# Square roots on ScalarE, two more merges on GpSimd and a new order, in a fused long-convolution and FFN kernel

## What is computed

```
q = layernorm(x)                                  # over the last axis, eps 1e-5
kv[b,i,j,h,l] = k[b,h,i,l] * k[b,h,j,l]           # k is the context; it is v too
y = causal convolution of kv along l with ssm_kernel[h]   (irfft(rfft(kv) * rfft(kernel)))
out = einsum('bijhl,bhil->bjhl', y + kv * D[h], q)
x = x + out
g = silu(W_gate layernorm(x));  u = W_up layernorm(x)     # W = (integer - 128) * scale
x = x + W_down (g * u)
```

## Time and profile before

| what | us |
|---|---|
| median of 3 runs | 76.36 |
| lowest and highest | 76.27, 76.8 |
| span of the profiled execution, first to last instruction | 74.54 (page: 74.5) |
| total of the profiled execution itself | not shown |

### The profile page before, as it was taken

The page is one execution under the profiler, slowest core; times in us unless marked ns, Lnnn a source line. Parts: engine busy times, 40 slices in busy tenths (PEclk is TensorE's granted clock), DMA queues, the critical chain, the costliest instruction groups (busy, mean ns, idle before and its releaser), DMA issues.

```text
span 74.5 us, 1494 instructions
## 1 busy us (share of the span) xinstructions
PE 69.8 (94%) x470; PEld 57.7 (77%) x470; DVE 61.7 (83%) x187; ACT 45.5 (61%) x115; POOL 58.8 (79%) x76
## 2 busy tenths in 40 slices
PE   5999989999999989999999999999999999999920
PEld 4666557988878848889798889797999989899810
DVE  0078899999988999999999899999968884586760
ACT  1503436464867879967746894657768796776400
POOL 6033587997999999899999999479998999339230
PEclk9999999999999999999999999999999999999998
DMA  0898999999997000000000000000002006000404
GB/s 8 235 254 230 372 315 364 324 382 392 361 356 224 29 0 0 0 0 4 9 0 0 0 0 4 0 0 0 0 13 70 0 0 210 1 9 0 140 1 141
DMA packets 7128, 8.29 MB, mean 111 GB/s; under 512 B 816, under 2 KB 6224, under 8 KB 7120
## 3 DMA queue, kind: packets, MB, share of 16 engines
q1 hardware_dynamic: 6768, 7.88, 33.0%
q10 hardware_dynamic: 352, 0.31, 1.2%
HBM read 7.12 MB, written 1.07 MB: 110 GB/s over the span
## 4 chain that ended last, share of the span: by engine, by line
PE 68%; POOL 16%; DVE 9%; issue 2%; ACT 1%; POOLq 0%; DVEq 0%
PE conv L1018 26%; PE down L1037 13%; POOL products L387 10%; PE conv L985 6%; PE turn L1058 5%; PE conv L994 5%; PE conv L996 5%; POOL rstd_q L371 4%; PE turn L965 3%; DVE terms L731 3%; PE turn L947 2%; PE turn L1037 2%; POOL terms L279 2%; DVE terms L734 1%; DVE terms L738 1%
## 5 line engine op out<-in xcount | busy, mean ns | idle before, releaser
L1018 PE MATMUL conv<-f_parts,wgu 128*128 128x256 f16 x176 | 22.1, 273 | 0.0
L387 POOL TENSOR_TENSOR products<-k_skip 128x512 f32<-128x512 f32 (+1 forms) x16 | 18.2, 1147 | 1.2 <-DMA k_skip<-ctx_skip 1.2
L1018 PEld LDWEIGHTS conv<-f_parts,wgu 128*128 128x128 f16 x176 | 16.6, 98 | 2.7 <-DVE hidden L746 0.2
L257 POOL TENSOR_TENSOR h_lo<-hidden,h_hi 128x256 fp32r<-128x256 f32 x18 | 13.1, 745 | 2.6 <-ACT h_hi L527 2.5
L746 DVE SCALAR_TENSOR_TENSOR hidden<-conv,su_sb,gate_act 128x256 f32<-128x256 f32 (+1 forms) x24 | 11.5, 482 | 3.0 <-ACT gate_act L522 2.8
L522 ACT ACTIVATE gate_act<-conv,sg_sb 128x256 f32<-128x256 f32 (+1 forms) x24 | 11.2, 467 | 4.2 <-PE conv L1018 3.9
L985 PE MATMUL conv<-products,toeplitz 128*128 128x288 f32 x32 | 11.3, 437 | 0.1
L731 DVE TENSOR_TENSOR terms<-conv,q_ext 128x512 f32<-128x512 f32 x16 | 10.9, 682 | 0.5 <-ACT q_ext L504 0.3
L994 PE MATMUL conv<-products,toeplitz 128*128 128x288 f32 x32 | 10.6, 413 | 0.3 <-DVE toeplitz L664 0.3
L996 PE MATMUL conv<-products,toeplitz 128*128 128x288 f32 x32 | 10.4, 406 | 0.0
L527 ACT ACTIVATE h_hi<-hidden 128x256 fp32r<-128x256 f32 x20 | 8.3, 413 | 3.4 <-DVE hidden L746 3.1
(11 more groups left out here) (64 smaller groups left out, 121.6 us busy)
## 6 DMA issues: line engine op xcount, KB each, us to landing
k_skip<-ctx_skip SPq DMA_DIRECT2D x3, 384.0 KB, 5.9
toeplitz<-taps_pad SPq DMA_DIRECT2D x2, 512.0 KB, 8.6
out<-x_sb SPq DMA_DIRECT2D x7, 128.0 KB, 1.7
toeplitz<-matrices SPq DMA_DIRECT2D x3, 256.0 KB, 5.4
wg_int<-wg_t SPq DMA_DIRECT2D x1, 704.0 KB, 7.6
wu_int<-wu_t SPq DMA_DIRECT2D x1, 704.0 KB, 8.8
wd_int<-wd_t SPq DMA_DIRECT2D x1, 640.0 KB, 10.0
x_sb<-x SPq DMA_DIRECT2D x1, 512.0 KB, 5.1
```

The source lines that it names most:

```text
L257: eng.tensor_tensor(low_of(i, t), hidden[up_lanes(t), i % 2, t, :], high_of(i, t), ALU.subtract).then_inc(done, 1)
L387: nc.gpsimd.tensor_tensor(view(products[:, n:n + 1], first * MADE + GROUP, [[MADE, halves], [GROUP, 4], [1, GROUP]]), view(k, 0, [[EXT * B ...
L1018: done = nc.tensor.matmul(bank_of(i, t)[:, n, :], wgu[:, c, column:column + P], f_parts[:, i % 2, part, c, :], start=(c == 0 and part == 0 ...
```

## The change

- The eight roots of q are taken by ScalarE's square root with eps as its bias, in four instructions (tiles 0, 1, 2 and 3, 4 to 7: `SQRT_Q`), followed by VectorE's reciprocal and one shift for each of these groups. The same holds for FFN tiles 0 and 1 (`SQRT_F`), with a shift of their own for each; GpSimd keeps the roots of FFN tiles 2 to 7. `variance_of_q` goes, and so does `variance_of_f` for tiles 0 and 1.
- ScalarE loads the square root's table at the start and Silu's between `squares(12)` and `squares(13)`, ahead of `gate(0, 0)`.
- Tile 1's front and back slots are merged on GpSimd, between `pairs(6)` and `pairs(7)`, so that its sum has 8 transposes instead of 16.
- The lists of all engines but SyncE's are in another order; `fill` has 17 matmuls instead of 18. Waits for loads stand inside the helpers now.
- GpSimd fills one more constant, eps.

The diff, cut; after what is shown the orders go on differing in the same way to the end of each list:

```diff
@@ -42,11 +42,14 @@
 HIGH_ON_DVE = []
 LOW_ON_DVE = [(LAST, 1), (LAST, 4)]
 
-UNMERGED = 2
-TWICE_MERGED = 3
-BACK_ON_POOL = [5, 6, 7]
+FRONT = {1: "pool", 2: "pool", 3: "pool", 4: "pool", 5: "pool", 6: "pool", 7: "pool"}
+BACKS = {1: "pool", 2: "dve", 3: "dve", 4: "dve", 5: "pool", 6: "pool", 7: "pool"}
+BOTH = {3: "dve", 4: "dve", 5: "dve", 6: "dve", 7: "dve"}
 
 EARLY_TURNS = 6
+
+SQRT_Q = [(0, 1), (1, 2), (2, 4), (4, TILES)]
+SQRT_F = [(0, 1), (1, 2)]
 
 
 
...
-TERM_SLOTS = [0, P, 2 * P, 3 * P, BACK, BACK + P + SPARE, BACK + 2 * (P + SPARE), CROSS]
-ONCE_SLOTS = [0, 2 * P, BACK, BACK + 2 * (P + SPARE)]
-TWICE_SLOTS = [0, BACK]
+FRONT_SLOTS = [0, P, 2 * P, 3 * P]
+BACK_SLOTS = [BACK, BACK + P + SPARE, BACK + 2 * (P + SPARE), CROSS]
+
+
+def slots_of(t):
+    if t in BOTH:
+        return [0, BACK]
+    front = FRONT_SLOTS[::2] if t in FRONT else FRONT_SLOTS
+    back = BACK_SLOTS[::2] if t in BACKS else BACK_SLOTS
+    return front + [BACK, BACK + 2 * (P + SPARE)] if t in BACKS else front + back
...
             pool.wait_ge(half_ready, 1)
-            root_q(0)
-            pool.wait_ge(k_loaded[2], 16)
             pairs(2, 0, 1)
             pairs(2, 1, 2)
-            root_q(1)
             pairs(3, 0, 1)
             pairs(3, 1, 2)
-            root_q(2)
-            pool.wait_ge(k_loaded[3], 16)
             pairs(4, 0, 2)
             pairs(5, 0, 2)
             pairs(6, 0, 2)
-            root_q(3)
+            merge_front(nc.gpsimd, 1)
+            merge_back(nc.gpsimd, 1)
             pairs(7, 0, 2)
-            root_f(0)
-            pool.wait_ge(k_loaded[4], 16)
             pairs(8, 0, 2)
+            pairs(9, 0, 2)
             merge_front(nc.gpsimd, 2)
-            root_q(4)
-            pairs(9, 0, 2)
-            root_f(1)
             pairs(10, 0, 2)
-            root_q(5)
             pairs(11, 0, 2)
-            pool.wait_ge(k_loaded[5], 16)
+            merge_front(nc.gpsimd, 3)
             pairs(12, 0, 2)
-            root_q(6)
-            merge_front(nc.gpsimd, 3)
-            root_q(7)
             merge_front(nc.gpsimd, 4)
-            low(0, 0)
             root_f(2)
             pairs(13, 0, 2)
+            low(0, 0)
+            pairs(14, 0, 2)
             root_f(3)
             low(0, 1)
+            merge_front(nc.gpsimd, 5)
+            merge_back(nc.gpsimd, 5)
+            pairs(15, 0, 2)
             low(0, 2)
-            pairs(14, 0, 2)
-            merge_front(nc.gpsimd, 5)
-            pairs(15, 0, 2)
...
+            def sqrt_q(n):
+                first, last = SQRT_Q[n]
+                act.wait_ge(q_moments, last)
+                nc.scalar.activation(std_q[:, first:last], moments_q[:, first:last, 1], ACT.Sqrt,
+                                     bias=eps[:, :]).then_inc(q_std, 1)
+
+            def sqrt_f(n):
+                first, last = SQRT_F[n]
+                act.wait_ge(f_moments, last)
+                nc.scalar.activation(std_f[:, first:last], moments_f[:, first:last, 1], ACT.Sqrt,
+                                     bias=eps[:, :]).then_inc(f_std, 1)
...
-            nc.scalar.preload_act_table(ACT.Silu)
+            nc.scalar.preload_act_table(ACT.Sqrt)
             act.wait_ge(taps_ready, 1)
             act.dma_start(taps_pad, taps_sb[:, :]).then_inc(taps_stored, 16)
+            act.wait_ge(eps_ready, 1)
+            sqrt_q(0)
             norm_q(0)
             evict_q(0)
-            act.wait_ge(k_loaded[2], 16)
+            sqrt_q(1)
             squares(2)
+            norm_q(1)
             squares(3)
-            norm_q(1)
+            squares(4)
+            evict_q(1)
+            squares(5)
             wrap(0)
-            evict_q(1)
-            act.wait_ge(k_loaded[3], 16)
-            squares(4)
+            sqrt_q(2)
             norm_q(2)
-            squares(5)
             squares(6)
             wrap(1)
+            squares(7)
+            squares(8)
+            norm_q(3)
             evict_q(2)
-            squares(7)
-            act.wait_ge(k_loaded[4], 16)
-            squares(8)
+            sqrt_q(3)
+            sqrt_f(0)
             convert_gate()
-            norm_q(3)
-            wrap(2)
-            squares(9)
             evict_q(3)
             norm_f(0)
+            squares(9)
             norm_q(4)
+            wrap(2)
+            high_f(0)
+            squares(10)
+            sqrt_f(1)
+            norm_q(5)
+            evict_q(4)
             convert_up()
-            squares(10)
-            high_f(0)
-            evict_q(4)
             norm_f(1)
+            wrap(3)
+            evict_q(5)
             squares(11)
-            wrap(3)
             high_f(1)
-            norm_q(5)
+            squares(12)
+            load_silu()
+            squares(13)
+            gate(0, 0)
+            squares(14)
+            wrap(4)
+            hidden_high(0, 0)
+            gate(0, 1)
+            norm_q(6)
             convert_down()
-            evict_q(5)
-            act.wait_ge(scales_loaded, 3 * 16)
-            gate(0, 0)
-            wrap(4)
-            gate(0, 1)
-            hidden_high(0, 0)
-            norm_q(6)
+            gate(0, 2)
...
+            def rstd_of_q(n):
+                first, last = SQRT_Q[n]
+                dve.wait_ge(q_std, n + 1)
+                dve.reciprocal(rstd_q[:, first:last], std_q[:, first:last]).then_inc(q_rstd, 1)
+
+            def shift_of_q(n):
+                first, last = SQRT_Q[n]
+                dve.wait_ge(q_rstd, n + 1)
+                dve.scalar_tensor_tensor(out=shift_q[:, first:last], in0=moments_q[:, first:last, 0], scalar=-1.0,
+                                         in1=rstd_q[:, first:last], op0=ALU.mult,
+                                         op1=ALU.mult).then_inc(q_shift, last - first)
...
+            def rstd_of_f(n):
+                first, last = SQRT_F[n]
+                dve.wait_ge(f_std, n + 1)
+                dve.reciprocal(rstd_f[:, first:last], std_f[:, first:last]).then_inc(f_rstd, last - first)
+
             def shift_of_f(t):
-                wait(dve, f_rstd, t + 1)
+                if t < len(SQRT_F):
+                    dve.wait_ge(f_rstd, t + 1)
+                else:
+                    wait(dve, pool_f_rstd, t + 1 - len(SQRT_F))
...
-            dve.wait_ge(x_loaded[0], 16)
+            all_products(0, 0, 1)
             stats_of_q(0)
-            dve.wait_ge(k_loaded[0], 16)
-            all_products(0, 0, 1)
             moments_of_q(0)
             all_products(0, 1, 2)
-            dve.wait_ge(anti_ready, 1)
-            dve.wait_ge(direct_loaded[0], 16)
             direct(0)
-            variance_of_q(0)
+            rstd_of_q(0)
             shift_of_q(0)
-            dve.wait_ge(k_loaded[1], 16)
             all_products(1, 0, 1)
+            direct(1)
             all_products(1, 1, 2)
-            dve.wait_ge(direct_loaded[1], 16)
-            direct(1)
-            dve.wait_ge(x_loaded[1], 16)
             stats_of_q(1)
             moments_of_q(1)
             multiply_terms(0)
-            variance_of_q(1)
-            dve.wait_ge(direct_loaded[2], 16)
+            rstd_of_q(1)
+            shift_of_q(1)
             direct(2)
+            multiply_terms(1)
+            stats_of_q(2)
+            stats_of_q(3)
             direct(3)
-            dve.wait_ge(x_loaded[2], 16)
-            stats_of_q(2)
-            shift_of_q(1)
             moments_of_q(2)
-            multiply_terms(1)
-            variance_of_q(2)
-            stats_of_q(3)
-            dve.wait_ge(direct_loaded[3], 16)
+            moments_of_q(3)
             direct(4)
+            multiply_terms(2)
+            rstd_of_q(2)
             direct(5)
             shift_of_q(2)
-            moments_of_q(3)
-            multiply_terms(2)
-            variance_of_q(3)
             multiply_terms(3)
+            stats_of_q(4)
             add_sum(0)
-            dve.wait_ge(x_loaded[3], 16)
-            stats_of_q(4)
-            stats_of_f(0)
+            direct(6)
+            stats_of_q(5)
             moments_of_q(4)
-            dve.wait_ge(direct_loaded[4], 16)
-            direct(6)
-            moments_of_f(0)
-            shift_of_q(3)
-            multiply_terms(4)
-            variance_of_f(0)
-            direct(7)
-            variance_of_q(4)
-            multiply_terms(5)
-            add_sum(1)
-            shift_of_f(0)
-            stats_of_q(5)
-            stats_of_f(1)
             stats_of_q(6)
             moments_of_q(5)
+            stats_of_q(7)
+            stats_of_f(0)
+            moments_of_q(6)
+            moments_of_q(7)
+            moments_of_f(0)
+            multiply_terms(4)
+            rstd_of_f(0)
+            rstd_of_q(3)
+            direct(7)
+            add_sum(1)
+            shift_of_q(3)
+            shift_of_f(0)
+            stats_of_f(1)
+            multiply_terms(5)
             moments_of_f(1)
+            multiply_terms(6)
             merge_back(dve, 2)
-            shift_of_q(4)
```

(104 more changed lines are left out.)

268 lines of the change are left out of this document (136 added, 132 removed).

## The result

| kernel | median, us | lowest to highest | runs |
|---|---|---|---|
| before | 76.55 | 76.27 to 76.8 | 4 |
| changed | 82.5 | 81.68 to 83.3 | 4 |

The ratio is 1.0746, with a 95% interval from 1.0674 to 1.0817: 6 us slower, where 1 us faster was forecast, and outside the range (74.7 to 76.6). The profiled execution is the slowest of the four (83.3 us, span 81.5); the fastest has a span of 79.9. The runs of the changed kernel spread over 1.6 us, those of the kernel before over 0.5. Ratios, and the comparison with `no_tile1`, use only the runs within 1.5% of the fastest of the same kernel, which leaves out the 83.3 here, one run of `after_nodirect` (80.07) and two of `no_tile1` (84.64 and 84.72, with a lower granted clock, 0.979).

A forecast was written before the change was run, and what follows sets the result against it. The prediction took TensorE as the bound, VectorE and GpSimd close behind. Terms +0.27 - 0.87 + 0.16 - 0.50, rounded to -1.0, and -0.05 for the rest gave 76.36 - 1.05 = 75.3 us, range 74.7 to 76.6.

The forecast's parts named there:

- the sentence on the roots: Ten roots off GpSimd: VectorE's net -0.7 us gains nothing by itself, only keeps VectorE behind TensorE.
- `direct(3)` ... 11.75: Head 3: `direct(3)`, put behind `multiply_terms(1)` and two statistics, ends at 11.75; TensorE's second part starts 0.27 us later.
- the sum of 8.9 us from 15.19 to `low_f(0)`: VectorE's work before the gates, at old durations, ends at 24.10, so TensorE waits 0.16 us.
- the port rule: GpSimd and a VectorE instruction with two SBUF inputs share ports; the later blocks; tile 1's merges would end 0.3 us later.
- tile 1's merges: Two GpSimd merges in series, 1.23 us each, end at 17.7, before TensorE arrives at 17.81: no wait.
- The eight transposes of tile 1's sum: Tile 1's sum on TensorE: 16 matmuls become 8, -0.87 us, the firm term.
- The 0.50 us for TensorE's wait at 27.15: TensorE waits there for VectorE's `low_f(0)`; the 0.50 us lost were counted as gained.
- The second table load: Silu's table on ScalarE before `gate(0, 0)`: 1.28 us, hidden by moved work; uncovered, up to 1.3 us.
- rival 2: The load of Silu's table isn't hidden and ScalarE drains around it: 76.1 us; chance 0.14.
- Rival 1: VectorE becomes the bound after the gates if its 0.7 us saving doesn't come: 75.9 us; chance 0.12.
- Rival 3: Tile 1's merges come late, the second ending after 18.7, and TensorE waits: 77.2 us; chance 0.10.
- Rival 4: The square root's table lacks Square, Identity or Copy, costing some ten more loads: 89 us; chance 0.02.

The follow-up runs named there:

- no_tile1: The changed kernel with tile 1's two merges on GpSimd taken out again (16 transposes in its sum): 83.74 us median of four; the two runs compared 82.84 and 82.85.
- after_nodirect: The changed kernel without VectorE's eight `direct` (D not added to the diagonal of heads 0 to 7): 79.48 us against 82.5.
- roots_only: The kernel before in its own order, with only the ten roots moved from GpSimd to ScalarE and VectorE: 79.77 us, ratio 1.043.
- roots_kept: roots_only with GpSimd's ten roots, results unused, and their variance instructions put back: 77.72 us, ratio 1.0164 to the kernel before.
- port_bench: VectorE and GpSimd alone, no kernel computation, in stages; 128-column VectorE instruction beside GpSimd adds: 1359 ns with two SBUF tensors, 343 with one in PSUM (stage 2).
- low_f_first: The kernel before with `low_f(0)` put ahead of `multiply_terms(7)` in VectorE's list: 76.57 us against 76.34, ratio 1.0039.
- low_f_start: low_f_first plus the changed kernel's start (head 0's first product ahead of the first statistics, 17 fill matmuls): 76.39 us against 76.34, ratio 1.0002.

## Why the prediction was wrong

**The step that failed** is the sentence on the roots: "This buys nothing by itself, it keeps VectorE behind TensorE." It took GpSimd's roots for load. They were also the times in which VectorE's two-tensor instructions ran. Everything after it used VectorE's durations of the kernel before ("`direct(2)` starts at 9.24", "`direct(3)` ... 11.75", the sum of 8.9 us from 15.19 to `low_f(0)`). Where the new lists put these instructions beside GpSimd's long ones, those durations don't hold. `roots_only` shows it (3.4 us from this edit alone), and so does `roots_kept` (2.05 of them back with useless roots).

**The rule was read one way only.** The prediction had the port rule, and said that "the later one blocks". It then priced GpSimd's waiting for VectorE ("by the rule the merges would end some 0.3 later") and not VectorE's waiting for GpSimd, which is the dear side: 1.0 us for each `direct` in port_bench, and 0.55, 0.71 and 0.85 for `direct(2)` to `direct(4)` in the changed kernel, against 0.3. The kernel before gave no instance of it, and that absence was the thing to ask about: some 20 two-tensor instructions on VectorE beside a GpSimd that is busy 79% of the time, and none of them late.

**The chain, step by step.** `norm_q(0)` started at 5.28 (forecast 5.54) and `multiply_terms(0)` at 7.60 (7.7): right. The shift of tile 1 took 0.62 and `direct(2)` 0.89: the first divergence, at 9.05. `direct(3)` ended at 13.39 (11.75), `multiply_terms(3)` at 17.59 (15.19), by waits of the shift (0.5 us) and of `direct` (0.89, 1.05 and 1.19 us instead of 0.34). VectorE was never idle between 7.60 and 17.59.

**The terms that were right.** A square root takes 0.28 to 0.30 us and a reciprocal 0.15, inside their bounds; tile 1's merges took 1.27 and 1.32, near the 1.23 used, and came late only because VectorE was late. The eight transposes of tile 1's sum took 1.06 us instead of 1.91, as forecast; what that brings to the whole kernel `no_tile1` is too close to tell.

**A term that was not.** The 0.50 us for TensorE's wait at 27.15 counted the wait as gained once `low_f(0)` came earlier. In `low_f_first` and `low_f_start` it did come earlier, and the wait moved to the next conv: neither kernel is faster than the one before.

**The second table load** was hidden, so rival 2 falls. ScalarE in the changed kernel:

```profile
31.19 0.30 ACT L492 ACTIVATE products<-k_skip 128x128 f32<-128x128 f32 x1
31.51 1.28 ACT L554 ACT_TABLE_LOAD   x1
32.80 0.31 ACT L492 ACTIVATE products<-k_skip 128x128 f32<-128x128 f32 x1
33.33 0.47 ACT L546 ACTIVATE gate_act<-conv,sg_sb 128x256 f32<-128x256 f32 x1 [0.22 <-PE conv L1056]
```

The load starts 0.02 us after the instruction before it has ended, the next one starts 0.01 after the load, and the gate waits for TensorE, not for the table. The Trainium skill (ScalarE: Activation LUTs, "What ACT_TABLE_LOAD costs") adds a drain of about 1.38 us to each switch; in this trace there is none, and the measurement decides.

**The rivals.** Rival 1 named the right engine (the chain that ended last runs over VectorE for 53%) and gave it a price of 0.6 us, because it counted instructions and not what stretches them. Rival 3 had the right sign and the wrong place. Its condition did come true, the second merge ended after 18.7 (at 20.2), but because `multiply_terms(3)` was 2.4 us late, and taking the merges out made the kernel no faster. Rival 4 was wrong: two table loads in all. The share given to slower, 0.12, covered the doubt about the terms that I had, not the doubt about the durations that I copied.

**Where the 6 us lie**: +3.4 from the roots off GpSimd (79.77 against 76.36), +3.1 from the new order and the grouped roots with the roots gone (82.84 against 79.77), -0.4 from tile 1's merges (82.47 against 82.84, less than the runs spread). These are steps from one kernel to the next, so their sum says nothing about the causes. Open remain the 1.4 us of `roots_kept` over the kernel before, and how much of the 3.1 isn't port waits. Reading the diagonal of `direct` from PSUM, for which stage 2 of port_bench speaks, has no measurement. A kernel was written for it (`direct_psum`: the changed kernel with the diagonal in spare columns of the PSUM bank `turn` and the shifts with a per-partition scalar, 2 to 4 us less expected), but nothing in it orders VectorE's write behind TensorE's matmuls into the same bank, and it gave no time.

## What to carry to other kernels

Before an instruction is taken from GpSimd, list VectorE's instructions with two SBUF tensors and what GpSimd does while each runs; a short instruction or a wait on GpSimd between long ones can be what lets VectorE through. If such instructions are never late in a trace, that is an alignment and has a price when either list moves; copy their durations only together with their neighbours. An operand in PSUM in place of a second SBUF tensor kept an instruction at its plain duration (343 ns, 128 columns), and so did a per-partition scalar (205 ns, measured on one column only).

## What the runs showed of the hardware

- VectorE with two SBUF tensors beside a stream of GpSimd adds of 1.26 us gets one instruction through for each add: it takes 1359 ns for 128 columns, where 343 is plain. GpSimd's adds pay almost nothing for it (1310 ns at most).
- A root of one column on GpSimd, 0.54 us long, doesn't hold up VectorE (685 ns beside it, 686 alone); GpSimd's root is the one that gets longer (606 on average, 1065 at most).
- More work can be faster: ten useless GpSimd instructions of 0.55 us, with their waits and ten more instructions of VectorE, made a kernel 2.05 us faster (79.77 to 77.72).
